# Single rows addressed in bytes, and a unit fetched by them every 12 chunks in place of every 16

## The reference

```python
n_in, n_out = node[recv], node[send]
wn_out = n_out @ W_lin + b_lin
e_ij = leaky_relu2(concat([n_in, n_out]) @ W_att + b_att)      # slope 0.2
a_ij = (e_ij @ w_alpha)[:, 0]
a_exp = exp(a_ij - segment_max(a_ij, recv)[recv])
alpha = a_exp / max(segment_sum(a_exp, recv)[recv], 1e-12)
n_i = segment_sum(alpha[:, None] * wn_out, recv)
x = layernorm(x + elu(n_i))
```

## Time and profile before

| | us |
|---|---|
| median of 3 runs | 2277.44 (2276.98 to 2277.66) |
| the profiled execution | 2278.64 |
| its span, first to last instruction | 2276.9 |
| the loop over chunks | from about 130 to 2229 |
| mean granted TensorE clock | 0.962 |

### The profile page before, as it was taken

How to read it: one execution, slowest core, us unless ns; L and a number is a source line. 1 busy time by engine, 2 the same in 40 slices (tenths; PEclk the granted TensorE clock), 3 DMA queues, 4 the chain that set the end, 5 groups by cost and what they waited for, 6 DMA issues and landing times.

```text
span 2276.9 us, 63415 instructions
## 1 busy us (share of the span) xinstructions
PE 1779.8 (78%) x11705; PEld 1440.8 (63%) x11705; DVE 1854.8 (81%) x5629; ACT 1471.6 (65%) x4913; POOL 1599.3 (70%) x1670
## 2 busy tenths in 40 slices
PE   5648798888878988887888878888788788877780
PEld 2336676666666766666666666666666666666660
DVE  9849998887789988887898888888767677667667
ACT  2326688876667766665666766676666666666655
POOL 2067777777777777777777777777777777777760
PEclk9869999999999999999999999999999999999995
DMA  3145555555555555555555555555555555555531
GB/s 122 61 113 138 136 138 136 132 133 140 128 135 132 138 133 135 132 138 130 135 132 132 132 138 134 132 136 133 135 137 136 133 137 134 136 134 136 134 105 57
DMA packets 165722, 294.16 MB, mean 129 GB/s; under 512 B 40002, under 2 KB 110014, under 8 KB 165329
## 3 DMA queue, kind: packets, MB, share of 16 engines
q0 software_dynamic: 78864, 216.03, 36.8%
q1 hardware_dynamic: 85733, 73.82, 12.6%
q10 hardware_dynamic: 732, 0.27, 0.1%
HBM read 278.95 MB, written 11.02 MB: 127 GB/s over the span
## 4 chain that ended last, share of the span: by engine, by line
POOL 23%; issue 13%; PE 8%; DVE 5%; DMA 4%; DVEq 1%; ACT 0%; POOLq 0%; ACTq 0%
POOL rows L651 23%; DMA rows<-qv_table,senders 4%; PE hidden_ps L967 2%; PE turned_ps L993 2%; PE masked_ps L978 2%; DVE sums L1581 1%; PE hidden_ps L965 1%; DVE leaky L1537 1%; PE turned_ps L985 1%; DVEq L1581 1%; PE masked_ps L977 0%; DVEq L435 0%; DVE spare L1672 0%; DVE x_sb L1667 0%; DVE keys L1145 0%
## 5 line engine op out<-in xcount | busy, mean ns | idle before, releaser
L651 POOL DMA_INDIRECT rows<-qv_table,senders x1635 | 1571.5, 961 | 498.9 <-issue 471.5
L993 PEld LDWEIGHTS turned_ps<-rows,spare 128*128 128x128 f32 x3270 | 441.8, 191 | 351.3 <-ACT spare L778 207.9
L965 PE MATMUL hidden_ps<-identf,rows 128*128 128x128 f32 x1635 | 461.7, 282 | 257.2 <-DMA rows<-qv_table,senders 242.0
L1581 DVE SCALAR_TENSOR_TENSOR sums<-sums,shrink,turned_ps 128x129 f32 x1660 | 572.7, 345 | 81.4 <-issue 38.4
L763 ACT ACTIVATE spare<-masked_ps,peaks 128x128 f32<-128x128 f32 x1660 | 474.4, 369 | 227.1 <-DVE peaks L1559 225.6
L967 PE MATMUL hidden_ps<-onehotT,p_unit 128*128 128x128 f32 x3320 | 592.4, 280 | 0.0
L993 PE MATMUL turned_ps<-rows,spare 128*128 128x129 f32 x3270 | 481.8, 279 | 114.5 <-DVE sums L1581 108.1
L967 PEld LDWEIGHTS hidden_ps<-onehotT,p_unit 128*128 128x128 f32 x3320 | 523.6, 198 | 0.9 <-issue 0.9
L1544 DVE TENSOR_REDUCE lows<-masked_ps 128x4 f32<-128x512 f32 x415 | 285.6, 688 | 275.9 <-PE masked_ps L978 274.7
L746 ACT ACTIVATE p_unit<-p_all 128x128 f32 x1660 | 400.5, 311 | 74.5 <-issue 50.8
L753 ACT ACTIVATE sloped<-hidden_ps 128x512 f32<-128x512 f32 x415 | 248.9, 600 | 282.8 <-PE hidden_ps L967 278.5
(11 more groups left out here) (202 smaller groups left out, 896.5 us busy)
## 6 DMA issues: line engine op xcount, KB each, us to landing
lanes_all<-lane_list SPq DMA_DIRECT2D x415, 128.0 KB
single_rows<-qv_table SPq DMA_DIRECT2D x3200, 1.0 KB
rows<-qv_table,senders POOLq DMA_INDIRECT x1635
qv_table<-rows SPq DMA_DIRECT2D x24, 257.0 KB, 2.7
out<-x_sb SPq DMA_DIRECT2D x1, 1344.0 KB
out<-x_sb SPq DMA_DIRECT2D x1, 896.0 KB
kept<-windows SPq DMA_DIRECT2D x3, 208.0 KB
out<-x_sb SPq DMA_DIRECT2D x1, 448.0 KB
```

The lines of the kernel that those rows point to most:

```text
L651: g.indirect_dma_start(out=rows[:, k % U, c, :], out_offset=None, in_=table, in_offset=bass.IndirectOffsetOnAxis(ap=senders[:, s % 2, c * ...
L965: t.matmul(whole[:, unit], rows_at_unit(k, c)[:, 0:F], identf[:], is_transpose=True, start=True, stop=False, skip_group_check=True)
L993: mm = t.matmul(unit_sums_ps[:, c, :], weights[:, k % 2, c * P:(c + 1) * P], rows_at_unit(k, c)[:, F:R], start=True, stop=True)
L1581: v.scalar_tensor_tensor(out=at, in0=at, scalar=shrink[:, k % 4, i:i + 1], in1=unit_sums_ps[:, i, :], op0=ALU.mult, op1=ALU.add).then_inc( ...
```

## The change

SP's table rows and the destination `single_rows` are seen as bytes (uint8), R x 4 = 1028 of them. `single_at` now holds the sender's number times 1028, so that the register is the address. ROW_CHUNKS is 12: the last unit of every 12th chunk is fetched by SP. The 16 groups of eight rows of a unit are spread over the 12 chunks by LOADS_TO = 0, 1, 2, 4, 5, 6, 8, 9, 10, 12, 13, 14, 16.

```diff
-    ROW_CHUNKS = -(-UNIT // ROWS_EACH)
+    ROW_CHUNKS = 12
+    LOADS_TO = [-(-UNIT // ROWS_EACH) * n // ROW_CHUNKS for n in range(ROW_CHUNKS + 1)]
...
-    flat_table = table.rearrange("n r -> (n r)")
+    BYTES = R * 4
+    table_bytes = table.bitcast(U8).rearrange("n r -> (n r)")
...
-                first = k % ROW_CHUNKS * ROWS_EACH
+                first, end = [ROWS_EACH * n for n in LOADS_TO[k % ROW_CHUNKS:k % ROW_CHUNKS + 2]]
...
-                for r in range(first, min(first + ROWS_EACH, UNIT), 8):
+                for r in range(first, end, ROWS_EACH):
                     starts = nc.values_load_multi_w_load_instructions(
-                        single_at[row:row + 1, s % 2, r:r + 8], engines=(mybir.EngineType.SP,), min_val=0,
-                        max_val=(PAD_ROW + P - 1) * R,
+                        single_at[row:row + 1, s % 2, r:r + ROWS_EACH], engines=(mybir.EngineType.SP,), min_val=0,
+                        max_val=(PAD_ROW + P - 1) * BYTES,
...
-                        sp.dma_start(single_rows[r + i:r + i + 1, n % RING_S, :],
-                                     flat_table[bass.ds(starts[i], R)].rearrange("(a r) -> a r", a=1)
+                        sp.dma_start(single_rows[r + i:r + i + 1, n % RING_S, :].bitcast(U8),
+                                     table_bytes[bass.ds(starts[i], BYTES)].rearrange("(a r) -> a r", a=1)
                                      ).then_inc(fetched_in(n)[0], 16)
...
-                    v.tensor_scalar(single_at[0:NO, s % 2, :], single_at[0:NO, s % 2, :], float(R), None,
+                    v.tensor_scalar(single_at[0:NO, s % 2, :], single_at[0:NO, s % 2, :], float(BYTES), None,
...
-                    v.tensor_scalar(single_at[:, s % 2, :], kept_i[:, (PER - 1) * UNIT:PER * UNIT], float(R), None,
+                    v.tensor_scalar(single_at[:, s % 2, :], kept_i[:, (PER - 1) * UNIT:PER * UNIT], float(BYTES), None,
```

More of the change, by code:

```diff
@@ L8 @@
 I32 = mybir.dt.int32
+U8 = mybir.dt.uint8
 ALU = mybir.AluOpType
@@ L562, in fetch_rows @@
                         sp.wait_ge(high_sums_done, single_of[n - RING_S] + 1)
-                for r in range(first, min(first + ROWS_EACH, UNIT), 8):
+                for r in range(first, end, ROWS_EACH):
                     starts = nc.values_load_multi_w_load_instructions(
-                        single_at[row:row + 1, s % 2, r:r + 8], engines=(mybir.EngineType.SP,), min_val=0,
-                        max_val=(PAD_ROW + P - 1) * R,
-                        skip_runtime_bounds_check_because="they are rows of the table, times the length of a row")[1]
-                    for i in range(8):
-                        sp.dma_start(single_rows[r + i:r + i + 1, n % RING_S, :],
-                                     flat_table[bass.ds(starts[i], R)].rearrange("(a r) -> a r", a=1)
+                        single_at[row:row + 1, s % 2, r:r + ROWS_EACH], engines=(mybir.EngineType.SP,), min_val=0,
+                        max_val=(PAD_ROW + P - 1) * BYTES,
+                        skip_runtime_bounds_check_because="they are rows of the table, times the bytes of a row")[1]
+                    for i in range(ROWS_EACH):
+                        sp.dma_start(single_rows[r + i:r + i + 1, n % RING_S, :].bitcast(U8),
+                                     table_bytes[bass.ds(starts[i], BYTES)].rearrange("(a r) -> a r", a=1)
                                      ).then_inc(fetched_in(n)[0], 16)
```

## The result

The changed kernel takes 2309.03 us (median of 4 runs, 2307.76 to 2310.72) where the kernel before takes 2277.21 beside it: a ratio of 1.0147, 95% interval 1.0134 to 1.016. It is slower by 32 us. The prediction said slower, by 94 us: the direction is right and the time lies in its range, but the size is a third of what was forecast.

The account below looks back on a forecast made before the run. POOL's gathers bound the kernel; SP would take over, its rows ending at 2278 (middle of 2282 and 2273), plus the closing part: 2322.5 against 2229.4, +93.1 us, so 2371 us; range 2264 to 2467.

Parts of the forecast that it names:

- What bounds the kernel now: POOL's gathers set the pace, 1.254 us start to start, from 129.9 to 2209.3 us; nine fewer give -11.3 us.
- ALU_OP goes, MOVE stays: Per row on SP, the product with 4 (33 ns) goes; the MOVE (29 ns) and the DMA issue (228 ns) stay.
- The row DMA as bytes costs 228 ns: SP's issue of a row as 1028 bytes was taken to cost 228 ns, as with 257 floats.
- SP becomes the bound from the first chunks on: SP needs 62.5 us per twelve chunks against POOL's 58.9 and starts with no lead; chance 0.70.
- The ALU_OP is worth 0.055 us, between 0.033 and 0.070: SP's saving per row without the product: 0.033 is itself alone, 0.070 adds a third of 0.110 us of handovers.
- My first sum: SP's loop as groups 1925.8, lists 163.2, short stops 37 and other issues 18: 2144 us, from 138.2 ending at 2282.
- The second way: SP's last row from today's 2120.4: less 184 of waits, plus 510 for nine units, less 176 of ALU_OPs, plus 3: 2273.
- The closing part: Behind SP's last row: 2.5 us landing, 26.3 for seven chunks at PE's pace, 15.7 from last hidden product to closing part.
- SP keeps up: Rival 1: the MOVE goes too or handovers shrink, so POOL still sets the pace; 2266 us, chance 0.20.
- The waits of SP that go: SP's waits for one-hots, the sort's keys and the pads, some 184 us in the loop, go as SP loses its lead.
- What was to be seen: Profile signs: eight rows in some 2.65 us, DVE and PE waiting some hundred us in all, POOL gaps over 0.3 us.
- Edits at nothing: The earlier ring wait, the changed constant in two products and the uneven groups were costed at nothing.

Follow-up runs that it names:

- SP free: Changed kernel, a unit every 12 chunks, but eight rows come with one DMA from a fixed table place, without a load of addresses: 2263.37 us.

## Why the prediction was right and wrong

- *What bounds the kernel now*: right. Taking nine gathers away with SP free gives 2263.4, and the six at 13 chunks 2269.65, as POOL's 1.254 us say.
- *ALU_OP goes, MOVE stays*: right, as the line's rows show.
- *The row DMA as bytes costs 228 ns*: right, 228 again: 4352 issues at the old median, and bytes alone made no difference of time. The Trainium skill (DMA: Bandwidth & Descriptors, "Why a DMA increments its semaphore by 16 and not by 1") says that software can split a contiguous row by its largest factor up to 16, here into 4 pieces. The packet counts, 85733 with floats and 85733 with bytes, show that it was not split here.
- *SP becomes the bound from the first chunks on*: right. Of DVE's 223.6 us of waiting for lists 25.4 lie before 400 us, in 12 waits, which is the share of the loop that has passed by then (262 of 2120 us): the lack is there from the start and doesn't grow.
- *The ALU_OP is worth 0.055 us, between 0.033 and 0.070*: this is the step that failed. It is 0.074, above my upper end. The working split the 0.172 us between two DMAs into the instructions and three handovers and gave the ALU_OP its own 0.033 and most of one handover. I had estimated two handovers at 0.03 and called the sum of 0.063 a little high, because a group's first issue might be long. The runs show that a register instruction costs over twice its record: 0.033 recorded, 0.074 paid. The one handover was about right (27 ns in the mean, 22 taken). What the working had at nothing is that the two handovers beside it shrink when the ALU_OP goes, by 15 ns together.
- *What follows for the sum*: a group cost 3.79 - 0.39 = 3.40 us in place of 3.54, and 544 x 0.14 = 76 us. My first sum ended SP's rows at 2282; with 3.40 it is 2206; measured 2214.4. Of the 8 us left, SP's waits before that point are +23.5, most of them 0.3 us long, which the sum had at nothing. The short stops took some 24 us (76 gaps by 0.31) where the sum had 37, and a list 0.39 where it had 0.40: together some -17. The second way had the same fault twice, in the nine units and in the ALU_OPs of the others: 2120.4 - 184 + 490 - 237 + 3 = 2192. It took off all of SP's waits, and the 23.5 that remained make it 2216.
- *Luck in the range*: its lower case for SP as the bound, 0.070 and 2306 us, is near the measured 2309 by chance. With the ALU_OP's true worth the forecast would have been about 2290, and the 23.5 us of waits left out are about the rest.
- *The closing part* of 2.5 + 26.3 + 15.7 = 44.5 us: right. The first instruction behind the loop, against the earlier trace rows:

```profile
2258.48 0.20 DVE L1653 TENSOR_SCALAR recip<-sums 128x49 f32<-128x49 f32 x1
```

2258.48 - 2214.4 = 44.1.

- *The size*: SP and POOL need 60.2 and 58.9 us for 12 chunks. The forecast rested on the difference of two near-equal sums, 62.5 and 58.9. An error of 4% in one made the difference wrong by a factor of three. I had written the point at which it turns, 0.079 per row; the product's worth, 0.074, is close to it. So the chance of 0.20 for "SP keeps up" looks too small beside a handover that had not been measured.
- *The waits of SP that go*: right, from 204.5, 24.7 and 12.2 us to 28.5, 0.8 and 1.7.
- *What was to be seen*: eight rows span 2.52 us where 2.65 was said, the same fault as above. DVE waits 223.6 us for lists and PE 8.2 for one-hots, where "some hundred us in all" was said. PE's 68.8 us for single rows were not foreseen; moving them away changed no time.
- *Edits at nothing*: whether the groups' order is one, one, two or two, one, one makes no difference, as the other spread shows. Neither the uneven groups nor the earlier wait for the ring can have held SP for more than its 23.5 us of waits, and none of these is for the ring.

## What to carry to other kernels

Where work is moved from one queue to another, make the sum of both queues per period, with loads, lists and stops, and look for the share at which they meet; here 13 chunks gain 0.26% and 12 lose 1.5% with the same code. Read the cost of a small instruction from the start-to-start interval over a whole group with and without it, not from its record. If the trace has no form without it, as here before the change, its record and an even share of the gaps are no upper end. And when a queue is the bound, a cheaper load of its addresses is worth as much as a cheaper row: sixteen addresses a load turned the loss of 1.5% into a gain of 0.5%.

## What the runs showed that I had not expected

- A register product recorded with 33 ns makes each row 74 ns longer (4352 of them, 323 us), and a fused one recorded with 35 ns 86 ns; a part of it lies in longer gaps beside the neighbouring instructions.
- SP stopped for some 0.3 us at every 128th of its instructions, in the changed kernel 76 times between 138 and 2214 us.
- A load of register values from SBUF took 0.732 us for eight and 1.186 us for 16, 0.057 us per value.
- Moving the landing of a unit's last rows forward, for which PE had waited 68.8 us, did not change the time (2309.07 for 2309.03 us).
